# Routing rows to experts at the end of a graph network: row squares on ScalarE, ranks summed by TensorE, seven expert tiles written out

## The reference

```python
x = x + _L1_gnn_ref(_layernorm(x, axis=-1), L1_gnn_W, L1_gnn_b, src, dst)
x = x + _L1_ffn_ref(_layernorm(x, axis=-1)[None], L1_ffn_W)[0]
...
BINS = [-1.5, -1.0, -0.5, 0.0, 0.5, 1.0, 1.5]
y = x[..., 0]
mem = jnp.sum(y[..., None] > BINS, axis=-1)      # which of 8 experts: the row's first number
for k in range(8):
    sel = (memf == k)[:, None].astype(x.dtype)
    out = out + sel * (xf @ W[k])                # W[k] is 512 x 512
```

## Time and profile before

| | |
|---|---|
| median of three runs | 1158.98 us |
| the profiled execution's own time | 1159.66 us |
| its span | 1157.8 us |
| mean granted TensorE clock | 0.982 |
| busy in the span: PE, PEld, DVE, ACT, POOL | 94%, 50%, 75%, 38%, 59% |
| share of the chain that ended last: PE, DVE, DMA, POOL | 56%, 18%, 10%, 6% |

### The profile page before, as it was taken

The page is one execution under the profiler, slowest core; times in us unless marked ns, Lnnn a source line. Parts: engine busy times, 40 slices in busy tenths (PEclk is TensorE's granted clock), DMA queues, the critical chain, the costliest instruction groups (busy, mean ns, idle before and its releaser), DMA issues.

```text
span 1157.8 us, 15265 instructions
## 1 busy us (share of the span) xinstructions
PE 1088.7 (94%) x3706; PEld 578.1 (50%) x3707; DVE 871.9 (75%) x2769; ACT 444.4 (38%) x1091; POOL 684.1 (59%) x758
## 2 busy tenths in 40 slices
PE   7989998489999999999999999999999999998797
PEld 3568887355444454444544544444445444343443
DVE  6747766769989988789798798797798786665411
ACT  3721114444444534434434434434433443441131
POOL 2010005477777777777777776777766777775322
PEclk9989999789999999999999999999999999999899
DMA  8960011499999999999999999999999999976432
GB/s 321 407 260 2 2 40 71 171 411 391 378 410 408 409 409 409 409 409 409 409 409 409 409 409 409 409 409 409 409 407 378 409 409 410 409 307 250 170 107 74
DMA packets 108664, 380.49 MB, mean 329 GB/s; under 512 B 11946, under 2 KB 12624, under 8 KB 108452
## 3 DMA queue, kind: packets, MB, share of 16 engines
q0 software_dynamic: 92352, 334.49, 72.9%
q1 hardware_dynamic: 16228, 45.04, 10.6%
HBM read 352.14 MB, written 28.46 MB: 329 GB/s over the span
## 4 chain that ended last, share of the span: by engine, by line
PE 56%; DVE 18%; DMA 10%; POOL 6%; issue 5%; DVEq 3%; ACT 2%; SPq 0%; POOLq 0%; ACTq 0%
PE tr L2098 26%; DMA big<-in_wdu,idx 10%; PE acc L1878 6%; DVE big L1531 5%; POOL big L701 4%; PE acc L1949 4%; PE tr L2190 4%; PE acc L1990 4%; PE acc L1960 2%; PE acc L1809 2%; POOL AT L701 1%; PE acc L1832 1%; DVE AT L1531 1%; DVE topi L1397 1%; PE tr L1982 1%
## 5 line engine op out<-in xcount | busy, mean ns | idle before, releaser
L701 POOL DMA_INDIRECT big<-in_wdu,idx x504 | 479.6, 952 | 184.9 <-issue 137.7
L2098 PE MATMUL tr<-big,back 128*128 128x512 f32 x1008 | 463.4, 599 | 14.0 <-ACT back L1039 13.6
L1531 DVE CUSTOM_DVE_ANT_0 big<-big,acc,prob 128x512 f32<-128x512 f32 x504 | 353.7, 742 | 82.1 <-DMA big<-in_wdu,idx 80.3
L1039 ACT ACTIVATE back<-ident,inner 128x128 f32<-128x128 f32 x576 | 199.4, 394 | 407.2 <-DVE inner L1531 407.1
L2098 PEld LDWEIGHTS tr<-big,back 128*128 128x128 f32 x1008 | 184.1, 190 | 249.3 <-issue 197.5
L701 POOL DMA_INDIRECT AT<-in_wdu,idx x124 | 118.3, 954 | 40.4 <-issue 34.7
L2098 PE MATMUL tr<-AT,back 128*128 128x512 f32 x248 | 115.1, 598 | 1.4 <-ACT back L1039 1.3
L1531 DVE CUSTOM_DVE_ANT_0 AT<-AT,acc,prob 128x512 f32<-128x512 f32 x124 | 87.3, 742 | 23.2 <-DMA AT<-in_wdu,idx 22.9
L1990 PE MATMUL acc<-front 128*128 128x512 f32 x188 | 90.7, 607 | 0.6 <-issue 0.5
L1878 PE MATMUL acc<-AT,big 128*128 128x256 f32 (+1 forms) x400 | 90.5, 377 | 0.0
L1949 PEld LDWEIGHTS acc<-front 128*128 128x128 f32 x640 | 78.0, 195 | 19.1 <-issue 17.1
(11 more groups left out here) (334 smaller groups left out, 1083.3 us busy)
## 6 DMA issues: line engine op xcount, KB each, us to landing
sorted_rows<-big SPq DMA_DIRECT2D x33, 640.0 KB, 18.7
big<-in_we SPq DMA_DIRECT2D x8, 1024.0 KB, 14.5
big<-in_wdu,idx POOLq DMA_INDIRECT x504, 9.1
x<-sorted_rows SPq DMA_DIRECT2D x14, 257.5 KB, 2.7
x<-in_x SPq DMA_DIRECT2D x1, 2304.0 KB
big<-in_xt SPq DMA_DIRECT2D x2, 1024.0 KB, 8.7
front<-in_wq SPq DMA_DIRECT2D x1, 2048.0 KB, 7.7
AT<-in_wdu,idx POOLq DMA_INDIRECT x124, 9.3
```

The lines of the kernel that those rows point to most:

```text
L701: pool.indirect_dma_start(out=k.slot[r * GS + s], out_offset=None, in_=k.wdu_d, in_offset=bass.IndirectOffsetOnAxis(ap=k.idx[i % 2][:, j:j ...
L1039: ins = act.activation(k.diag[:, c * P:(c + 1) * P], to, ACT.Relu, scale=k.inner[:, j:j + 1])
L1531: ins = dve.tensor_tensor_reduce(out=row, in0=row, in1=k.Y[i % 2] if i < NT - 1 else k.Yh[j // WIDTH], scale=k.prob[:, (i % 2) * HK + j:(i ...
L2098: ins = pe.matmul(k.O[i % 2], k.diag[:, c:c + P], row, start=(g == 0 and s == 0), stop=(g == groups_of(i) - 1 and s == GS - 1))
```

## The change

- `stats` and `bn_aggr` go. DVE's x3 instruction also writes the row's sum (`accum_out`), and ACT works out the negated mean and the sum of squared differences (`row_squares`, `ACT.Square` with `accum_out`). The root's scale takes the division by 512.
- `lt8`, a 128x64 comparison, moves ahead of DVE's `x_add` of the last tile.
- The batches are (0, 4), (4, 7), (7, 10). POOL and DVE no longer make `cnt`; TensorE sums `sel` of all earlier tiles (`earlier`). Batch 0 is scaled after x3 of tile 4 and placed after tile 5; batch 1 is scaled after tile 7 and placed after tile 9.
- The totals of tiles 0 to 6 stand ahead of the last ranks, those of tiles 7 to 9 behind them. The two `unread` ahead go, and seven stand behind where nine stood.
- The expert stage has seven tiles written out, with a buffer of their own each, and loops of three. It starts on `places_ready`. Three banks and three buffers take turns. `flip_z(m+1)` stands between the second and third matmul of `expert(m)`, and `value_load` ahead of the waits. A count of tiles is rounded up to 7 + 3n.

The diff, cut to its core:

```diff
-XR = 4
+EARLY_TILES, XR, PER_ROUND = 7, 7, 3
+LATE_AT = XR - PER_ROUND
...
-BATCHES = [(0, 5), (5, 7), (7, NT)]
-RANKED = {8: 0, 9: 1}
+BATCHES = [(0, 4), (4, 7), (7, NT)]
+SCALES_AFTER = {4: 0, 7: 1}
+PLACED_AFTER = {5: 0}
...
+def part_of(m):
+
+    return (m + 2) % 3
...
+    for m in range(EARLY_TILES):
+        at = firsts[m] if m < 4 else place(m)
+        sp.dma_start(k.xb[m], k.zs_d[bass.ds(at * P, P), :]).then_inc(k.loaded[m], 16)
...
+    with sp.Fori(FIRST_ROUND, rounds) as q:
+        for i in range(PER_ROUND):
+            at = place(q * PER_ROUND + (LATE_AT + i))
+            sp.wait_ge(k.x4_done, q * PER_ROUND + (2 + i))
+            sp.dma_start(k.xb[LATE_AT + i], k.zs_d[bass.ds(at * P, P), :]).then_inc(k.loaded[LATE_AT + i], 16)
...
+    def row_squares(t):
+        less_mean = k.mv[:, t:t + 1]
+        act.wait_ge(k.x3_done, t + 1)
+        act.activation(less_mean, k.rsum[:, t:t + 1], copy, scale=-1.0 / D)
+        act.drain()
+        if t >= 2:
+            act.wait_ge(k.var4_ready, t - 1)
+        act.activation(k.squares[t % 2], k.zx[t][:, 0:D], ACT.Square, bias=less_mean,
+                       accum_out=k.mv[:, NT + t:NT + t + 1]).then_inc(k.var4_ready, 1)
+
     for a, b in BATCHES:
+        for t in range(a, b):
+            row_squares(t)
         act.wait_ge(k.var4_ready, b)
...
+    lt8 = k.lt8.rearrange("p (a b) -> p a b", a=BINS)
+    dve.tensor_tensor(lt8, k.iota8[:, :].unsqueeze(1).to_broadcast([P, BINS, BINS]),
+                      k.iota8[:, :].unsqueeze(2).to_broadcast([P, BINS, BINS]), ALU.is_lt)
     x_add(NT - 1)
...
-                                 k.x[:, t * D:(t + 1) * D], ALU.mult, ALU.add).then_inc(k.x3_done, 1)
-        dve.drain()
-        stats(k.zx[t][:, 0:D], t)
...
+                                 k.x[:, t * D:(t + 1) * D], ALU.mult, ALU.add,
+                                 accum_out=k.rsum[:, t:t + 1]).then_inc(k.x3_done, 1)
+        if t in SCALES_AFTER:
+            scaled(SCALES_AFTER[t])
+        if t in PLACED_AFTER:
+            placed(PLACED_AFTER[t])
+    placed(1)
+    scaled(len(BATCHES) - 1)
     placed(len(BATCHES) - 1)
...
+    def earlier(n, tiles, begin):
+
+        b = BATCHES[n][1]
+        for t in tiles:
+            c = max(BATCHES[n][0], t + 1)
+            ins = pe.matmul(k.RK[0][:, c * BINS:b * BINS].rearrange("p (t b) -> p t b", b=BINS), k.ones1,
+                            k.sel[:, t * BINS:(t + 1) * BINS].unsqueeze(1).to_broadcast([P, b - c, BINS]),
+                            start=begin and t == 0, stop=(t == b - 2))
+        return ins
+
     def ranks(n):
         a, b = BATCHES[n]
-        pe.wait_ge(k.sel_ready, n + 1)
         if n:
             pe.wait_ge(k.pos_ready, n)
+            earlier(n, range(a), True)
         else:
             pe.wait_ge(k.e_consts, 1)
...
+        pe.matmul(k.RK[0][:, a * BINS:b * BINS], k.upper, k.sel[:, a * BINS:b * BINS], start=(n == 0), stop=False)
+        earlier(n, range(a, b - 1), False).then_inc(k.rank_psum, 1)
...
+        if t == 6:
+            ranks(0)
...
     ranks(1)
+    totals(range(BATCHES[-1][0]))
+    ranks(2)
+    totals(range(*BATCHES[-1])).then_inc(k.rank_psum, 1)
     pe.wait_ge(k.x3_done, 6)
-    unread(k.F[5], k.g[(NT - 1) % 3], 2)
-    last_ranks()
-    unread(k.F[5], k.g[(NT - 1) % 3], 9)
+    unread(k.F[5], k.g[(NT - 1) % 3], 7)
...
+    def expert(m, part, freed, then):
+
+        at = k.bini[0:1, m:m + 1] if isinstance(m, int) else k.bini[0:1, bass.ds(m, 1)]
+        b = pe.value_load(at, min_val=0, max_val=BINS - 1)
+        pe.wait_ge(k.zT_done, m + 1)
+        if freed is not None:
+            pe.wait_ge(k.x4_done, freed)
+        times_expert(part, b, 0)
+        times_expert(part, b, 1)
+        if then is not None:
+            flip_z(*then)
+        times_expert(part, b, 2)
+        times_expert(part, b, 3).then_inc(k.e_ready, 1)
+
+    pe.wait_ge(k.places_ready, 1)
+    flip_z(0, part_of(0))
+    for m in range(EARLY_TILES - 1):
+        expert(m, part_of(m), m - 2 if m >= 3 else None, (m + 1, part_of(m + 1)))
...
+    with pe.Fori(FIRST_ROUND, rounds) as q:
+        for i in range(PER_ROUND):
+            m = q * PER_ROUND + (LATE_AT + i)
+            expert(q * PER_ROUND + (3 + i), (i + 2) % 3, q * PER_ROUND + (1 + i), (m, i))
+    expert(pe.snap(rounds * PER_ROUND + 3), 2, pe.snap(rounds * PER_ROUND + 1), None)
```

More of the change, by code:

```diff
@@ L261, in lay_out @@
     k.ones1 = k.y[:, P:2 * P]
-    k.xb = [k.x[:, r * NPAD:r * NPAD + ROW] for r in range(XR)]
+    k.xb = [k.x[:, r * ROW:(r + 1) * ROW] for r in range(XR)]
     k.ob = [k.outT[:, r * D:(r + 1) * D] for r in range(XR)]
-    k.zT = [k.yT, k.gt]
-    k.zn = [k.h1bc[:, 0:D], k.h1bc[:, D:2 * D]]
+    k.zT = [k.yT, k.gt, k.back[:, 0:D]]
+    k.zn = [k.h1bc[:, 0:D], k.h1bc[:, D:2 * D], k.back[:, D:2 * D]]
+    k.squares = [k.sca, k.yT]
     k.ident = sb("ident", P)
@@ L759, in store @@
                                 oob_is_err=False).then_inc(k.stored[r], 16)
+    for m in range(EARLY_TILES):
+        store(m, m)
     pool.wait_ge(k.rounds_ready, 1)
     rounds = pool.value_load(k.rounds[0:1, 0:1], min_val=FEWEST, max_val=ROUNDS)
[L763 to L769, removed]
+    with pool.Fori(FIRST_ROUND, rounds) as q:
+        for i in range(PER_ROUND):
+            store(q * PER_ROUND + (LATE_AT + i), LATE_AT + i)
 def words_of(eng, k, w):
@@ L1078, in norm_z, with copy_zT @@
                        scale=k.xb[r][:, D:D + 1]).then_inc(k.zn_ready, 1)
[L1080 removed]
+    def copy_zT(m, part):
         act.wait_ge(k.zt_ready, m + 1)
[L1082 removed]
+        act.activation(k.zT[part][:, :], k.ZB[part], copy).then_inc(k.zT_done, 1)
+    for m in range(EARLY_TILES):
+        if m >= 2:
+            norm_z(m, part_of(m), m, 16)
+        copy_zT(m, part_of(m))
     act.wait_ge(k.rounds_ready, 1)
     rounds = act.value_load(k.rounds[0:1, 0:1], min_val=FEWEST, max_val=ROUNDS)
[L1086 removed]
@@ L1647, in binned @@
                           k.mem[:, a:b].unsqueeze(2).to_broadcast([P, b - a, BINS]), ALU.is_equal).then_inc(k.sel_ready, 1)
-    def runs(a, b, n):
-        dve.wait_ge(k.runs_ready, n)
-        for t in range(a, b):
-            dve.drain()
-            dve.tensor_tensor(k.cnt[:, (t + 1) * BINS:(t + 2) * BINS], k.cnt[:, t * BINS:(t + 1) * BINS],
-                              k.sel[:, t * BINS:(t + 1) * BINS], ALU.add)
-        dve.drain().then_inc(k.runs_ready, 1)
     def placed(n):
@@ L2161, in pe_program, with totals @@
+        pe.wait_ge(k.sel_ready, n + 1)
+        pe.matmul(k.RK[0][:, a * BINS:b * BINS], k.upper, k.sel[:, a * BINS:b * BINS], start=(n == 0), stop=False)
+        earlier(n, range(a, b - 1), False).then_inc(k.rank_psum, 1)
+    def totals(tiles):
+        for t in tiles:
+            ins = pe.matmul(k.RK[1][:, 0:BINS], k.ones1, k.sel[:, t * BINS:(t + 1) * BINS], start=(t == 0), stop=(t == NT - 1))
+        return ins
     for t in range(NT):
@@ L2203, in pe_program @@
-    with pe.Fori(last, full) as q:
-        for r in range(XR):
-            if r + 1 < XR:
-                flip_z(q * XR + r + 1, r + 1)
-            expert(q * XR + r, r)
-    with pe.Fori(full, rounds) as q:
-        for r in range(XR // 2):
-            flip_z(q * XR + r, r)
-        for r in range(XR // 2):
-            expert(q * XR + r, r)
+    with pe.Fori(FIRST_ROUND, rounds) as q:
+        for i in range(PER_ROUND):
+            m = q * PER_ROUND + (LATE_AT + i)
+            expert(q * PER_ROUND + (3 + i), (i + 2) % 3, q * PER_ROUND + (1 + i), (m, i))
```

182 lines of the change are left out of this document (51 added, 131 removed).

## The result

The changed kernel took 1151.41 us (median of 4 runs, 1150.23 to 1152.45) where the kernel before took 1159.78 beside it (4 runs, 1158.82 to 1161.17): a ratio of 0.9925, 95% interval 0.9913 to 0.9938. It is faster by 8.4 us. The prediction was 1148.8, with a range of 1145.3 to 1153.3; the point is 2.6 us too low. The kernel before had a median of 1158.98 us when the prediction was made and 1159.78 here, which is 0.8 us of these 2.6. The profiled execution took 1151.4, its span 1149.2.

The account below looks back on a forecast made before the run. Only the tail counts: x3 with TensorE and DVE level, a chain of short steps, then TensorE-bound experts. -4.4 - 1.5 - 4.9 + 0.6 = -10.2 us, from a median of 1158.98 to 1148.8 us; range 1145.3 to 1153.3.

Parts of the forecast that it names:

- x3 and the ranks: Tail up to the last ranks: x3 at TensorE's pace, ranks ready sooner; -4.4 us, with ends -6.8 and -2.3.
- S: The moment the last ranks lie in PSUM: predicted 1079.4 us, against 1083.8 before.
- the 24 matmuls: TensorE's small matmuls from 1071.6 us to the last ranks: 11 at 0.22, 13 at 0.41, 7.7 us.
- S to the first expert: From last ranks to first expert matmul: fewer totals, flip and register read off the path; -1.5 us, at least -0.4.
- The expert stage: Expert matmuls to the last pass: 13 tiles, 3.87 us each, one tile and a 1.0 us stop saved; -4.9 us.
- The slack of a flip's copy: Inside an expert tile: spare time before a flip's copy would delay the next expert, put at 0.9 us.
- The clock at the first expert: TensorE's clock after the unread matmuls, as experts begin: no fall assumed, 0 us.
- the other end named: At the first expert, the alternative to no clock fall: a loss of 1.8 us.
- its own sign of being wrong: In the next profile's first expert tile: clock 0.50 would speak against the prediction.
- The end: After the last pass: the last store now carries rows, so its landing takes longer; +0.6 us (0 to +1.4).
- Costs taken as nothing: Put at zero: moved `lt8` (1.06 us if uncovered), accumulator read (at most 0.1), seven buffers, removed `cnt` work, round count.

Follow-up runs that it names:

- dve_stats: The changed kernel with row statistics back on VectorE and no squares on ScalarE; against the changed kernel its median grew by 5.0 us, its tail by 7.0.
- flips_ahead: The changed kernel with the next tile's flip ahead of each expert and the register read behind the waits; tail 5.7 to 5.9 us longer than the changed kernel's.
- totals_behind: The changed kernel with all ten totals behind the last ranks, the same 27 small matmuls reordered; tail about 1.0 us longer than the changed kernel's.
- experts_only: The kernel before with only the new expert stage, its statistics, ranks, totals and unread matmuls kept; tail 5.2 us and median 4.2 us below the kernel before.
- one_more_round: The changed kernel with one round more than the rows need, 16 tiles and not 13; median and tail each grew by 11.3 us.
- counts_clock: The changed kernel with VectorE summing earlier selections (12 small matmuls, not 27) and unread matmuls filling TensorE's pauses; median 1147.04 us.
- clock_held: The changed kernel with one more unread pair behind the totals and one between the first flip and first expert; median 1147.92 us.

## Why the prediction was right, and what it mis-sized

- **x3 and the ranks, -4.4.** Right: S was 1079.19 (predicted 1079.4), so -4.6. x3 ran at TensorE's pace. ScalarE's last root stood at 1074.10, as worked out. The clock fell in the middle of the small matmuls, as taken from the earlier trace rows. That S came so close is in part luck: the 24 matmuls began 0.5 us later than worked out (1072.10) and took 7.05 us, not 7.7, and the two errors nearly cancel. What the sum did not see is that late selections can stop TensorE among the dense matmuls (dve_stats).
- **S to the first expert, -1.5.** Measured -1.3 (12.56 us, before 13.86). The totals come 0.33 us sooner behind S (put at 0.4), the two chains of VectorE and SP 0.18, and the stretch from the first load's issue to the first expert fell from 5.59 to 4.80 us, by 0.79, where 1.1 was put for the flip and the register read. These rows of the kernel before show what stood between the end of the first copy (1096.54) and the matmul:

```profile
1096.63 0.66 PE L2181 MATMUL acc<-ident,front 128*128 128x128 f32 x4 [0.72 <-DVE front L1750]
1097.69 3.70 PE L2190 MATMUL tr<-big,front 128*128 x8 [0.41 <-issue]
```

The 1.15 us are the second flip (0.66), 0.41 put down to issue, where the register read stands, and two short steps, as the prediction said. In the changed kernel 0.14 us stand there (the copy ends at 1091.61), so 1.0 us was won; its load and normalization took 0.2 us longer. flips_ahead, which puts the flip back, gives back 0.65. totals_behind moves all seven early totals and so prices their order in the changed kernel at about 1.0, more than the 0.4 of this step.

- **The expert stage, -4.9.** Right in every part: 13 tiles, 3.87 a period behind the first, no stop. The slack of a flip's copy was put at 0.9 us, which its own pieces don't give: 1.72 less 0.60 is 1.1, and the trace has 1.1 (a copy ends at 1100.36, the next expert's passes begin at 1101.45). The stage took 51.87 us (before 55.09), which is 50.1 and the clock's 1.77. experts_only gives 5.2 us by itself and one_more_round the price of a tile.
- **The clock at the first expert, 0: this step failed.** "Mine lies between; I take no fall, 0 us." It fell: 3.25 + 0.85 us for four passes and a flip where full speed gives 1.88 + 0.44, 1.8 us. That was the other end named. The prediction compared its stretch, 0.7 us of flips in the 3.5 us from 1088.4 to 1091.9, with two of the earlier trace rows, and said that it lies between them. It does not: the stretch with half clock behind it had 0.65 us of work in 2.7 us, so 2.05 idle, and 0.7 in 3.5 is 2.8 idle. The trace has 0.63 us of flip in the 2.63 us from 1089.13 to 1091.75, nearly that very stretch, with idle times of 1.22 and 0.78 us. So its own rows spoke for the fall, and its own sign of being wrong, a low clock in the first expert tile, came. The Trainium skill, "TensorE: Matmul & The Clock Gate", section "HAM oscillation", tells of a kernel in which TensorE waits for loads between short bursts of matmuls and every burst starts cold. Its waits are longer than the pauses here; the trace agrees in kind (clock 0.58 behind the two pauses, 1.00 where either was filled).
- **The end, +0.6.** Measured +0.55.
- **Costs taken as nothing.** `lt8` took 0.94 us ahead of the addition and hid in VectorE's idle time. The code up to the addition came 0.29 us later than before, within what profiles of unchanged code differ by.
The terms add up: -4.64 (S), -1.30, -3.22 (stage with the clock) and +0.55 are -8.61, and the span went from 1157.8 to 1149.2.

## What to carry to other kernels

Where TensorE waits for a load just ahead of a long run of matmuls, put its work and its pauses beside stretches of the same trace behind which the clock is known: here the trace of before held a stretch nearly alike. One pair of useless matmuls in either pause kept the clock, worth some 2 us of the tail, and the pair in the first pause delayed nothing. Giving work to an idle engine can be worth more than its duration, when the engine relieved would otherwise make TensorE wait in the middle of dense work, as one profiled execution of dve_stats shows. When a stage is shortened, look at the chain again: after the small matmuls came the scatters.

## What was not expected of the hardware

- TensorE counted as busy for 2.00 of 2.00 us with small matmuls, and its clock fell to 0.50 all the same (1076 to 1078). In counts_clock, where they came in two stretches of 0.8 and 1.7 us with 512-column matmuls ahead of and behind each, it stayed at 1.00.
- `lt8`, 64 elements wide and without a wait in front of it, took 0.94 us beside GpSimd's additions, as it took 1.06 before; other operations of that width took 0.2 (L1691, 80 wide, 0.24).
- The landing of a reload in the loop was 2.5 to 2.8 us in the changed kernel and 4.2 once in clock_held; that one late landing was enough to stop TensorE for 0.48 us. One of 3.6 in one_more_round stopped nothing.
